# A decoder layer on one core: k and v of linear attention in a bank each, rows turned before the numerators, and v's copy and the gate's maxima in other slots of cross attention

## The chip, the cores and the metric

One core of a Trainium2 chip runs the whole program. The metric is the device time of one execution in microseconds. The kernel before took 587.42, 587.35 and 584.94 us in three runs, a median of 587.35.

## What is computed

The reference, cut to what matters (128 batches of 64 tokens, 128 features, 16 heads of 8; each block sits in a residual sum with a norm):

```python
# linear attention, then a feed-forward part whose activation is looked up on a grid of 0.1
h = _layernorm(x, ln1_g, ln1_b)
q, k, v = (h @ wq), (h @ wk), (h @ wv)             # each split in 16 heads
phi_q = jax.nn.elu(q) + 1.0
phi_k = jax.nn.elu(k) + 1.0
kv = jnp.einsum('bshd,bshe->bhde', phi_k, v)
z = jnp.sum(phi_k, axis=1)
out = (num / den).reshape(B, S, D)                 # num = phi_q kv, den = phi_q z + 1e-6
x = x + out @ wo
x = x + _lookup_act(_layernorm(x, ln2_g, ln2_b) @ w1) @ w2
# cross attention over ctx with a causal mask and a mask of query rows
scores = jnp.einsum('bhqd,bhkd->bhqk', q, k) / SQRT_DK
attn = jax.nn.softmax(jnp.where(m != 0, NEG, scores), axis=-1)
x = _layernorm(x + jnp.einsum('bhqk,bhkd->bqhd', attn, v).reshape(b, s, d) @ WO)
# shared expert plus a second expert weighted by the renormalised two best gates
out = xf @ W_shared.T + (w0 + w1) * (xf @ W_expert.T) + bias
x = _layernorm(x + out)
```

## The kernel before

The 8192 tokens are 64 tiles of 128 rows, in 16 groups (`NG`) of four tiles (`TG`). Everything stays in SBUF between three stages: `phase1` is linear attention, `phase2` the feed-forward part, `phase3` cross attention and the experts. Each stage is a software pipeline written out by hand: `pipeline(engine, phase)` calls the phase for step s = -1 to 16 and beyond on each of the five engines, and a step works on several groups at once (g = s + 1 is being opened, s is worked on, r = s - 1 or s - 2 is being closed). Each engine runs its own list in order; semaphores tie the lists together (`wait_ge`, and `after`, which leaves the wait out for a count of zero). PSUM has eight banks, `bank(i)`, in four pairs.

**Linear attention, one step.** TensorE's order is: turn the finished attention of group s - 1 (bank 0); the kv sums of s (`kv_products`, L1067, banks 2 and 3); q of g (L1125, bank 1); the numerators of s (`numerators`, L1083, banks 4 and 5); turn the normed rows of s + 2 (`xpose_rows`, L1054, bank 0); k and v of g by one product of 256 columns a tile (L1136), in banks 6 and 7 together, two tiles in each; the output projection of r (L1145, bank 1). VectorE masks the sums (`kv_sum`, L833), divides (`attend`, L844 to L850), makes phi_q (L877, reads bank 1), takes the minimum of Exp(k) and 1 (L881), makes phi_k (L887, reads k in PSUM, and waits also for v's copy, since v lies in the same banks), and takes the next group's statistics (L290, L297). ScalarE copies the projection and the turned attention, takes Relu and Exp of q, makes hT from the turned rows (L587), takes Exp of k (L634) and copies v (L638), both once `kv_done` says that all four products are there. GpSimd adds the residual and norms the rows.

**Cross attention, one step.** Four slots, one a tile; the tiles are alternately wide (64 keys a query, even slots) and narrow (32 keys, odd slots). In each slot TensorE closes the scores of the tile after (`scores_close`, L1213), turns the tile's probabilities (`turn_probabilities`, L1245), opens the scores of the tile two on (`scores_open`, L1231; it waits for ScalarE's copy of the turned probabilities, since it takes over their banks) and weighs the values (`weigh_values`, L1257, L1264, L1273). Between these stand: in slot 0 the fourth expert product of s - 2 (`moe`, L1301; it waits for the first collect, whose bank 5 it takes), the turning of y of g (bank 4), k of g (L1282, bank 5), the turning of the attention of r (L1345, bank 6); in slot 1 the output projection of r (L1328, bank 6) and q of g (bank 4); in slot 2 v of g (`project_v`, L1293, bank 4); in slot 3 the turning of y2 of r (bank 6) and, last, expert products 0 to 2 of r, in banks 5, 4 and 6 (`MOE_BANK`). These three wait for y2's copy, for v's copy out of bank 4 and for k's copy out of bank 5.

ScalarE's slot: copy the tile's turned probabilities (`copy_pT`, L726), then the exponentials of the next tile (`probabilities`, L719, which wait for VectorE). Around these: in slot 0 first the fourth collect (`collect`, L733) and y's copy (`copy_y`, L687), then the turned probabilities, then k's copy (L699) and the attention's (L755); in slot 1 last q's copy (L693); in slot 2 the gate's Exp (L750) and last v's copy (`copy_v`, L707); in slot 3 y2's copy (L759), the exponentials, and then collects 0 to 2.

VectorE's slot: `shift` of the next tile (its scores' maxima, L934, and their subtraction, L940 or L947), then `xattend` of this tile (L922, L924), which waits for its weighed values. Around these: in slot 1 the residual sum (L1017), its statistics, and the gate's maxima (`gate_top`, L956 to L961; it waits for all four collects of s - 2); in slot 2 first the mask rows of g (`future_keys`, L1004), later the gate's weights; in slot 3 the experts' mixture (L992) and the last norm's statistics. GpSimd: spread k over the heads (`spread_k`, L514), add the bias, norm y2 (L327), spread v (`spread_v`, L526), norm the output. SyncE loads mask rows and ctx two groups ahead (the mask load waits for `future_ready` of the step before) and stores the output.

Of the kernel before, what the change touches and what calls it, by code (L numbers as in the profile page):

```python
# [44 lines left out]
MOE_BANK = [5, 4, 6, 5]  # L45
# [7 lines left out]
def decoder_layer(nc, x, ctx, mask, mask_early, ln1_g, ln1_b, wq, wk, wv, wo, ln2_g, ln2_b, w1, w2,  # L53
# [15 lines left out]
    with es:  # L69
# [132 lines left out]
        q_done, kv_done = sem("q_done"), sem("kv_done")  # L202
# [375 lines left out]
        def _(act):  # L578
# [25 lines left out]
            def phase1(s, p):  # L604
# [25 lines left out]
                if exists(g):  # L630
                    act.wait_ge(kv_done, g + 1)
                    after(act, phik_ready, g - 1)
                    kv = pair[3][:, :, :].rearrange("p a (t c) -> p (a t) c", c=2 * D)
                    nc.scalar.activation(expqk[q][:, 1, :].rearrange("p (t d) -> p t d", d=D),  # L634
                                         kv[:, :, 0:D], ACT.Exp).then_inc(expk_ready, 1)

# [3 lines left out]
                        kv[:, :, D:2 * D].rearrange("p t (h e) -> p t h e", e=DH), ACT.Copy)\  # L640
# [96 lines left out]
            def phase3(s, p, slots=range(TG)):  # L737
                nxt, prev, q = s + 1, s - 1, 1 - p
                for t in slots:
                    if t == 0 and exists(s - 2):  # L740
                        collect((s - 2) * TG + TG - 1, TG - 1, p)
                    if t == 0 and exists(nxt):
                        copy_y(nxt)
                    if exists(s):
                        copy_pT(s * TG + t, t % 2)
# [10 lines left out]
                    if t == TG - 1 and exists(prev):  # L756
                        act.wait_ge(y2_xposed, prev + 1)
                        after(act, moe_done, prev * TG)
                        nc.scalar.activation(y2T[:, :], bank(6), ACT.Copy).then_inc(y2T_ready, 1)  # L759
                    if exists(s) if t < TG - 1 else exists(nxt):  # L760
                        probabilities(s * TG + t + 1)
# [5 lines left out]
                    if t == 2 and exists(nxt):  # L767
                        copy_v(nxt, q)
# [26 lines left out]
        def _(dve):  # L795
# [68 lines left out]
            def phase1(s, p):  # L864
# [9 lines left out]
                if exists(g):  # L874
# [9 lines left out]
                    dve.wait_ge(v_ready, g + 1)  # L884
                    after(dve, kvsum_done, g - 1)
                    kv = pair[3][:, :, :].rearrange("p a (t c) -> p (a t) c", c=2 * D)
                    nc.vector.scalar_tensor_tensor(  # L887
                        phi_k[q][:, :, :], kv[:, :, 0:D], 1.0,
                        expqk[q][:, 1, :].rearrange("p (t d) -> p t d", d=D), ALU.add, ALU.max)\
                        .then_inc(phik_ready, 1)  # L890
# [117 lines left out]
            def phase3(s, p, slots=range(TG)):  # L1008
                prev, old, q = s - 1, s - 2, 1 - p
                for t in slots:  # L1010
                    if t == 2 and exists(s + 1):
                        future_keys(s + 1, q)
# [12 lines left out]
                    if t == 1 and exists(old):  # L1025
                        dve.wait_ge(moe_ready, (s - 1) * TG)
                        gate_top(old, p)
                    if t == 2 and exists(old):
# [11 lines left out]
            phase3(-1, 1, slots=(2, 3))  # L1040
# [7 lines left out]
        def _(pe):  # L1048
# [3 lines left out]
            def transposes(src, dst, done):  # L1052
                for t in range(TG):
                    last = nc.tensor.transpose(dst[:, P * t:P * (t + 1)], src[:, t, :], ident[:, :])  # L1054
                last.then_inc(done, 1)

# [359 lines left out]
```

## Time and profile before

| What | Value |
|---|---|
| Median of three runs | 587.35 us (584.94 to 587.42) |
| The profiled execution | 587.63 us, its span 585.9 us |
| Busy share of the span | PE 88%, weight loads 62%, VectorE 71%, ScalarE 61%, GpSimd 59% |
| Chain that ended last | PE 51%, VectorE 26%, "issue" 10%, ScalarE 9% |
| Linear attention | about 9 to 137 us |
| Feed-forward part | about 125 to 254 us |
| Cross attention and experts | about 254 to 586 us |

The three stages have different limits, so the shares of the whole span say little; the rows of one step are read instead. PE is TensorE's matmul, PEld its weight load. An fp32 product appears as two records. In a timeline a bracket at the end of a row tells how long the engine stood idle before it and who ended that; rows of one engine can overlap by about 0.1 us, since each includes its own drain.

### The profile page before, as it was taken

To read this page: it belongs to the slowest core of one execution; us is meant where nothing else is said; L and a number is where in the kernel's file an instruction comes from. 1 tells how busy PE (TensorE), PEld (TensorE's weight loads), DVE (VectorE), ACT (ScalarE), POOL (GpSimd) and SP (SyncE) were. 2 spreads that over 40 slices of the span, in tenths; PEclk is the share of its full clock that TensorE was granted. 3 is DMA by queue.
4 is the path that set the end of the run, shared out by engine and by line. 5 is a ranking of instruction groups with operands and counts; after the bars stand their busy time and mean duration, and the time that the engine had idled before them with its cause. 6 is when DMAs were issued, how large, how long until landed. Compare 5 with 4: busy or idle time off the path is not lost.

```text
span 585.9 us, 23209 instructions
## 1 busy us (share of the span) xinstructions
PE 515.8 (88%) x9440; PEld 365.5 (62%) x9440; DVE 417.7 (71%) x1468; ACT 358.2 (61%) x643; POOL 346.4 (59%) x666
## 2 busy tenths in 40 slices
PE   3799999898999999988999999999999999998741
PEld 1566666665777777665666666666666666766530
DVE  2677677765777667556768787889888898888843
ACT  2455565556777777747657666666667666666420
POOL 6566666645577766631546557565766567665463
PEclk9999999999999999998999899999999999999875
DMA  5530000000000000010101012101111021100001
GB/s 160 163 109 3 2 2 2 2 2 1 2 0 2 2 2 2 0 30 29 32 3 45 5 50 49 47 8 45 48 49 32 20 49 48 48 21 4 22 18 36
DMA packets 24730, 17.45 MB, mean 30 GB/s; under 512 B 2096, under 2 KB 22448, under 8 KB 24624
## 3 DMA queue, kind: packets, MB, share of 16 engines
q1 hardware_dynamic: 24192, 15.90, 9.7%
q8 instruction: 75, 1.23, 0.9%
q14 instruction: 31, 0.25, 0.2%
q10 hardware_dynamic: 432, 0.07, 0.1%
HBM read 11.77 MB, written 4.19 MB: 27 GB/s over the span
## 4 chain that ended last, share of the span: by engine, by line
PE 51%; DVE 26%; issue 10%; ACT 9%; POOL 1%; DVEq 1%; DMA 1%; POOLq 0%; ACTq 0%
PE pair L1199 9%; PE pair L1163 9%; PE pair L1301 7%; DVE neg_max L934 5%; PE pair L1136 5%; PE pair L1054 5%; DVE gel L947 4%; PE pair L1213 3%; DVE stats_b L290 3%; PE pair L1245 3%; DVE stats L290 2%; PE pair L1282 2%; ACT v L707 2%; PE pair L1083 2%; PE pair L1273 2%
## 5 line engine op out<-in xcount | busy, mean ns | idle before, releaser
L719 ACT ACTIVATE gel<-gel,row_scale 128x512 f32<-128x512 f32 x96 | 66.0, 718 | 55.8 <-DVE gel L947 31.4
L726 ACT ACTIVATE gel<-pair 128x1024 f32<-128x1024 f32 x64 | 51.9, 811 | 42.7 <-PE pair L1245 42.3
L1213 PE MATMUL pair<-k_exp,qT 32*32 32x128 f32 (+1 forms) x2048 | 68.5, 328 | 0.0
L1199 PEld LDWEIGHTS pair<-w,gel 128*128 128x128 f32 x512 | 60.4, 192 | 8.0 <-issue 5.7
L1199 PE MATMUL pair<-w,gel 128*128 128x128 f32 x512 | 62.5, 276 | 1.0 <-ACT gel L652 1.0
L934 DVE TENSOR_REDUCE neg_max<-pair 128x16 f32<-128x1024 f32 x64 | 60.9, 951 | 1.8 <-PE pair L1213 1.5
L1245 PE MATMUL pair<-ident,gel 128*128 128x128 f32 x384 | 56.4, 283 | 5.9 <-ACT gel L719 5.9
L1163 PE MATMUL pair<-hT,w 128*128 128x512 f32 x128 | 58.2, 595 | 1.3 <-ACT lev L647 1.3
L1245 PEld LDWEIGHTS pair<-ident,gel 128*128 128x128 f32 x384 | 42.5, 143 | 23.4 <-ACT gel L719 13.2
L514 POOL TENSOR_SCALAR k_exp<-k_sb,quad_mask 128x512 f32<-128x512 f32 x64 | 43.0, 690 | 12.2 <-ACT k_sb L699 6.7
L305 POOL TENSOR_SCALAR veps_b<-mv_b 128x4 f32<-128x4 f32 x32 | 7.7, 242 | 65.0 <-DVE mv_b L297 32.1
L1054 PE MATMUL pair<-ident,xn 128*128 128x128 f32 x192 | 31.6, 290 | 15.7 <-POOL xn L327 15.7
L947 DVE TENSOR_TENSOR gel<-pair,neg_max 128x512 f32<-128x512 f32 x64 | 41.2, 686 | 1.1
L526 POOL COPY v<-v 32x256 f32<-32x256 f32 x64 | 26.2, 409 | 26.3 <-ACT v L707 23.4
L491 POOL TENSOR_TENSOR X<-X,proj_sb 128x512 f32<-128x512 f32 x16 | 20.3, 1270 | 36.1 <-ACT proj_sb L609 36.1
L922 DVE RECIPROCAL rec<-pair 128x16 f32<-128x16 f32 x64 | 15.9, 248 | 36.1 <-PE pair L1273 34.4
L1301 PE MATMUL pair<-w_moe,y2T 128*128 128x263 f32 x128 | 40.6, 448 | 0.7 <-ACT y2T L759 0.7
L1163 PEld LDWEIGHTS pair<-hT,w 128*128 128x128 f32 x128 | 22.9, 190 | 23.8 <-issue 23.5
L305 POOL TENSOR_SCALAR veps_c<-mv_c 128x4 f32<-128x4 f32 x16 | 3.7, 228 | 55.4 <-DVE mv_c L297 44.9
L652 ACT ACTIVATE gel<-lev 128x512 f32<-128x512 int8 x64 | 36.3, 620 | 0.1
L307 POOL TENSOR_TENSOR rstd_b<-veps_b,minus_half 128x4 f32<-128x4 f32 x32 | 34.6, 1082 | 2.7
L290 DVE BATCH_NORM_STATS2 stats<-X 128x6 f32<-128x128 f32 x128 | 27.6, 280 | 10.6 <-DMA X<-in_x 10.6
(127 smaller groups left out, 1251.9 us busy)
## 6 DMA issues: line engine op xcount, KB each, us to landing
X<-in_x SPq DMA_DIRECT2D x16, 256.0 KB, 3.1
cT<-in_ctx SPq DMA_DIRECT2D x16, 256.0 KB, 3.8
out_rows<-X SPq DMA_DIRECT2D x16, 256.0 KB, 2.5
mask_rows<-in_mask_early SPq DMA_DIRECT2D x16, 128.0 KB, 3.9
w<-in_L_attn_w SPq DMA_DIRECT2D x2, 256.0 KB, 3.4
w_kv<-in_L_attn_wk SPq DMA_DIRECT2D x1, 64.0 KB, 2.9
w_kv<-in_L_attn_wv SPq DMA_DIRECT2D x1, 64.0 KB, 2.6
w_q<-in_L_attn_wq ACTq DMA_DIRECT2D x1, 64.0 KB, 2.8
```

What stands on the lines that cost most here:

```text
L290: last = nc.vector.bn_stats(stats[:, t, :], rows(t))
L514: last = nc.gpsimd.tensor_scalar(k_exp[q][:, h, :], k_sb[:, :], quad_mask[:, h:h + 1], 0.0, ALU.mult, ALU.add)
L719: nc.scalar.activation(part, part, ACT.Exp, scale=row_scale[:, n:n + 1])\
L726: nc.scalar.activation(pT[par], flat[:, 0:GW] if n % 2 else flat, ACT.Copy)\
L934: nc.vector.tensor_reduce(neg_max[par][:, :].rearrange("p (a h) -> p a h", a=2), scores, AX.X, ALU.max, negate=True).then_inc(max_ready, 1)
L947: nc.vector.tensor_tensor(rows[:, heads, :], scores[:, half, :, :], neg_max[par][:, heads].unsqueeze(2).broadcast_to([P, HH, S]), ALU.add) ...
L1054: last = nc.tensor.transpose(dst[:, P * t:P * (t + 1)], src[:, t, :], ident[:, :])
L1163: nc.tensor.matmul(bank(up_bank(s, f)), w_1[:, P * f:P * (f + 1)], hT[p][:, :], start=True, stop=True).then_inc(up_done, 1)
L1199: last = nc.tensor.matmul(bank(6 + q)[:, P * t:P * (t + 1)], gel[:, q, f, P * t:P * (t + 1)], w_2[:, f, :], start=(f == 0), stop=(f == NF ...
L1213: last = nc.tensor.matmul(pair[t % 2][b * QW:(b + 1) * QW, quad // 2, heads], qT[p][rows, batch + first:batch + first + QW], k_exp[p][rows ...
L1245: last = nc.tensor.transpose(flat[:, P * i:P * (i + 1)], probability_rows(n)[:, P * i:P * (i + 1)], ident[:, :])
L1301: nc.tensor.matmul(bank(MOE_BANK[t])[:, 0:2 * D + NE], y2T[:, P * t:P * (t + 1)], w_moe[:, :], start=True, stop=True).then_inc(moe_done, 1)
```

## The change

On linear attention: k and v are made by two sets of four products of 128 columns, k in bank 6 and v in bank 7, with a semaphore each. Exp(k) waits for k alone, v's copy for v, and phi_k no longer waits for v's copy. The rows of s + 2 are turned before the numerators of s. On cross attention: TensorE turns slot 0's probabilities before y; ScalarE copies the turned probabilities before y; v's copy moves from the end of slot 2 to slot 3, behind y2's copy and before the exponentials; VectorE takes the gate's maxima and the mask rows in slot 0, between the next tile's shift and the attend, instead of slots 1 and 2; expert products 1 and 2 swap banks 4 and 6, and only the third waits for v's copy. The waits that guard banks 4 and 6 in slot 0 swap their counts.

```diff
-MOE_BANK = [5, 4, 6, 5]
+MOE_BANK = [5, 6, 4, 5]
 ...
@@ ScalarE, phase1
-                    act.wait_ge(kv_done, g + 1)
+                    act.wait_ge(k_done, g + 1)
                     after(act, phik_ready, g - 1)
-                    kv = pair[3][:, :, :].rearrange("p a (t c) -> p (a t) c", c=2 * D)
-                    nc.scalar.activation(expqk[q][:, 1, :].rearrange("p (t d) -> p t d", d=D),
-                                         kv[:, :, 0:D], ACT.Exp).then_inc(expk_ready, 1)
-
+                    nc.scalar.activation(expqk[q][:, 1, :], bank(6), ACT.Exp)\
+                        .then_inc(expk_ready, 1)
+                    act.wait_ge(v_done, g + 1)
                     after(act, kvsum_done, g - 1)
                     nc.scalar.activation(
                         v_ext[q].rearrange("p t (h e) -> p t h e", e=HV)[:, :, :, 0:DH],
-                        kv[:, :, D:2 * D].rearrange("p t (h e) -> p t h e", e=DH), ACT.Copy)\
+                        bank(7).rearrange("p (t h e) -> p t h e", t=TG, e=DH), ACT.Copy)\
                         .then_inc(v_ready, 1)
@@ ScalarE, phase3
+                    if exists(s):
+                        copy_pT(s * TG + t, t % 2)
                     if t == 0 and exists(nxt):
                         copy_y(nxt)
-                    if exists(s):
-                        copy_pT(s * TG + t, t % 2)
 ...
+                    if t == TG - 1 and exists(nxt):
+                        copy_v(nxt, q)
                     if exists(s) if t < TG - 1 else exists(nxt):
                         probabilities(s * TG + t + 1)
 ...
-                    if t == 2 and exists(nxt):
-                        copy_v(nxt, q)
@@ VectorE, phase1
                     dve.wait_ge(mink_ready, g + 1)
-                    dve.wait_ge(v_ready, g + 1)
                     after(dve, kvsum_done, g - 1)
-                    kv = pair[3][:, :, :].rearrange("p a (t c) -> p (a t) c", c=2 * D)
                     nc.vector.scalar_tensor_tensor(
-                        phi_k[q][:, :, :], kv[:, :, 0:D], 1.0,
-                        expqk[q][:, 1, :].rearrange("p (t d) -> p t d", d=D), ALU.add, ALU.max)\
-                        .then_inc(phik_ready, 1)
+                        phi_k[q].rearrange("p t d -> p (t d)"), bank(6), 1.0, expqk[q][:, 1, :],
+                        ALU.add, ALU.max).then_inc(phik_ready, 1)
@@ VectorE, phase3
-                    if t == 2 and exists(s + 1):
-                        future_keys(s + 1, q)
 ...
-                    if t == 1 and exists(old):
+                    if t == 0 and exists(old):
                         dve.wait_ge(moe_ready, (s - 1) * TG)
                         gate_top(old, p)
+                    if t == 0 and exists(s + 1):
+                        future_keys(s + 1, q)
 ...
-            phase3(-1, 1, slots=(2, 3))
+            future_keys(0, 0)
+            phase3(-1, 1, slots=(3,))
@@ TensorE, phase1
+            def rows_product(dst, src, w):
+                for t in range(TG):
+                    last = nc.tensor.matmul(dst[:, P * t:P * (t + 1)], src[:, P * t:P * (t + 1)], w,
+                                            start=True, stop=True)
+                return last
 ...
-                if exists(s):
-                    numerators(s, p)
                 if exists(s + 2):
                     xpose_rows(s + 2, p)
                 if s + 2 == NG:
                     xpose_rows2(0, p)
+                if exists(s):
+                    numerators(s, p)
                 if exists(g):
                     after(pe, phik_ready, g)
-                    for t in range(TG):
-                        last = nc.tensor.matmul(
-                            pair[3][:, t // 2, 2 * D * (t % 2):2 * D * (t % 2 + 1)],
-                            hT[q][:, P * t:P * (t + 1)], w_kv[:, :], start=True, stop=True)
-                    last.then_inc(kv_done, 1)
+                    rows_product(bank(6), hT[q], w_kv[:, 0:D]).then_inc(k_done, 1)
+                    after(pe, v_ready, g)
+                    rows_product(bank(7), hT[q], w_kv[:, D:2 * D]).then_inc(v_done, 1)
@@ TensorE, phase3
-                    if t == 0 and exists(g):
-                        after(pe, moe_ready, (s - 1) * TG - 2)
-                        after(pe, v2_ready, g)
-                        turn_y(g)
                     if s == 0 and t == 0:
                         scores_close(1)
                     if exists(s):
                         turn_probabilities(s * TG + t, t)
+                    if t == 0 and exists(g):
+                        after(pe, moe_ready, (s - 1) * TG - 1)
+                        after(pe, v2_ready, g)
+                        turn_y(g)
 ...
                         pe.wait_ge(xatt_ready, r * TG + TG)
-                        after(pe, moe_ready, (s - 1) * TG - 1)
+                        after(pe, moe_ready, (s - 1) * TG - 2)
 ...
                         if exists(g):
-                            pe.wait_ge(v2_ready, g + 1)
                             pe.wait_ge(k_ready, g + 1)
                         for u in range(TG - 1):
+                            if u == 2 and exists(g):
+                                pe.wait_ge(v2_ready, g + 1)
                             moe(r, u)
```

## Rows read from the trace of the kernel before

**Rows 1.** Busy times of one cross-attention step: us, engines, PEclk (granted clock), DMA
```profile
388.72:407.39 18.67, 17.52 (x457) 12.19 (x456) 15.62 (x54) 12.29 (x23) 11.94 (x23) 1.00 0.14 40
```

**Rows 2.** The chain of waits, its longest pieces: start, length, work
```profile
21.71 1.74 PE pair L1136 x8
...
120.97 1.74 PE pair L1136 x8
...
292.29 1.53 PE pair L1301 x6
...
310.97 1.53 PE pair L1301 x6
...
349.89 1.53 PE pair L1301 x6
...
536.67 1.53 PE pair L1301 x6
```

**Rows 3.** Timeline of a linear-attention step: start, length, engine, line, work, idle before
```profile
95.32 0.69 DVE L887 SCALAR_TENSOR_TENSOR arena<-pair,arena 128x512 f32<-128x512 f32 x1
...
96.73 1.12 PE L1125 MATMUL pair<-hT,w_q 128*128 128x512 f32 x2
...
97.34 0.73 DVE L833 TENSOR_TENSOR arena<-pair,head_mask 128x576 f32<-128x576 f32 x1
...
98.12 0.73 PE L1083 MATMUL pair<-arena 64*64 64x72 f32 x32 [0.27 <-DVE arena L833]
...
98.78 0.66 PE L1054 MATMUL pair<-ident,xn 128*128 128x128 f32 x4
...
99.28 1.89 PE L1136 MATMUL pair<-w_kv,hT 128*128 128x256 f32 x8
...
100.44 0.68 DVE L877 SCALAR_TENSOR_TENSOR arena<-pair,arena 128x512 f32<-128x512 f32 x1
...
101.23 1.13 PE L1145 MATMUL pair<-w_o,attT 128*128 128x128 f32 x8
...
101.84 0.43 DVE L881 TENSOR_SCALAR arena<-arena 128x512 f32<-128x512 f32 x1 [0.71 <-ACT arena L634]
...
102.19 0.60 PE L1054 MATMUL pair<-ident,att 128*128 128x128 f32 x4
```

**Rows 4.** Timeline of a cross-attention step, from the fourth expert product on
```profile
389.09 0.71 PE L1301 MATMUL pair<-w_moe,y2T 128*128 128x263 f32 x2
...
389.84 0.39 ACT L733 ACTIVATE moe_out<-pair 128x263 f32<-128x263 f32 x1 [0.39 <-PE pair L1301]
...
393.98 0.26 DVE L922 RECIPROCAL rec<-pair 128x16 f32<-128x16 f32 x1 [1.61 <-PE pair L1273]
...
399.29 0.34 DVE L956 MAX8 top<-moe_out 128x8 f32<-128x8 f32 x4
...
400.73 0.68 DVE L934 TENSOR_REDUCE neg_max<-pair 128x16 f32<-128x512 f32 x1
...
401.31 1.73 POOL L327 TENSOR_SCALAR xn<-X,negm_b,rstd_b 128x128 f32<-128x128 f32 x4 [0.18 <-POOL negm_b L322]
...
402.80 1.26 ACT L707 ACTIVATE v<-pair 64x512 f32<-64x512 f32 x2
...
402.95 0.66 PE L1245 MATMUL pair<-ident,gel 128*128 128x128 f32 x4 [0.42 <-ACT gel L719]
...
404.09 0.60 ACT L726 ACTIVATE gel<-pair 128x512 f32<-128x512 f32 x1
...
404.58 0.59 ACT L759 ACTIVATE y2T<-pair 128x512 f32<-128x512 f32 x1
...
404.74 0.30 PE L1231 MATMUL pair<-causal_bf,ident_bf 32*32 32x256 bf16 x8 [0.70 <-ACT gel L726]
...
405.95 1.33 ACT L719 ACTIVATE gel<-gel,row_scale 128x512 f32<-128x512 f32 x2 [0.78 <-DVE gel L947]
```

**Rows 5.** Busy times and granted clock where the clock fell, as [rows 1]
```profile
329.70:332.70 3.00, 3.00 (x38) 2.11 (x27) 2.57 (x11) 2.09 (x4) 0.06 (x1) 0.56 0.01 3
```

More of the change, by code:

```diff
@@ L201, in decoder_layer @@
         xn_xposed, hT_ready = sem("xn_xposed"), sem("hT_ready")
-        q_done, kv_done = sem("q_done"), sem("kv_done")
+        q_done, k_done, v_done = sem("q_done"), sem("k_done"), sem("v_done")
         expq_ready, expk_ready, v_ready = sem("expq_ready"), sem("expk_ready"), sem("v_ready")
@@ L1143, in phase1 @@
                     after(pe, projsb_ready, r)
-                    for t in range(TG):
-                        last = nc.tensor.matmul(bank(1)[:, P * t:P * (t + 1)],
-                                                attT[:, P * t:P * (t + 1)], w_o[:, :],
-                                                start=True, stop=True)
-                    last.then_inc(proj_done, 1)
+                    rows_product(bank(1), attT, w_o[:, :]).then_inc(proj_done, 1)
                 if s + 2 == NG + 1:
```

## The prediction

> **What bounds the kernel now.** I read the busy shares of one step of cross attention first [rows 1], then the chain of waits for the places where its pattern repeats [rows 2], then the timeline of one step in each of the two stages that the diff touches [rows 3, 4]. In linear attention TensorE and VectorE both stand idle in every step (the brackets in [rows 3]), so a loop through several engines sets the pace. In one step of cross attention (388.72 to 407.39) TensorE is busy 17.5 of 18.67 us: the most that orders and waits can give back there is the rest, 1.1 us. The feed-forward stage between them is untouched.
>
> The k/v products stand on the chain once a group: from 21.71 to 120.97 us, 14 periods of 7.09 us [rows 2]. The loop in [rows 3]: numerators (98.12), rows turned (98.78), k/v products (99.28, 1.89 us), ScalarE's Exp of k (inside the 0.67 us from the products' end, 101.17, to the minimum), VectorE's minimum (101.84, having stood idle 0.71 us for that Exp), phi_k, the next statistics, kv_sum (97.34 in this period), numerators. In cross attention the shared expert products stand on the chain at 292.29 and, 13 steps on, at 536.67: 244.4 us. One of the 13 held a fall of the clock [rows 5], worth 1.6 us (below); the others take (244.4 - 1.6)/13 = 18.67 us. TensorE stands idle twice in such a step, 0.42 us ahead of turning slot 3's probabilities and 0.70 us ahead of opening the next scores [rows 4].
>
> **Part 1: k and v in a bank each, rows turned before numerators.** The eight 256-column records become sixteen of 128 columns. Eight such records with stationary 128x128 are in the rows: the output projection runs from 101.23 to the next matmul at 102.19, 0.96 us. The old form takes at most 101.23 - 99.28 = 1.95 us, some of which is a wait for phi_q (it ends 101.12). So k is ready after about 1.1 us with its drain in place of 1.89, v after 2 x 0.96 = 1.92. TensorE pays between 0 and 0.25 us a step; I take 0.2 and it lies in a wait, as follows.
>
> Count from the start of the numerators, n (98.12). VectorE ends phi_q at 101.12, n + 3.0, whatever happens to k: its den, reciprocal and att hang on the numerators alone. k's Exp is now done by then: numerators 0.66, k 1.1, Exp and its waits 0.67, together n + 2.4 (ScalarE comes to it after the hT copy, which also moves forward with the turned rows). The 0.71 us of idle go. What is late next: the projection needs phi_q's bank, so it starts at n + 3.11 as now; k and v, from n + 0.66 to n + 2.6, fit ahead of it. Then 0.96 to the turned attention (n + 4.07), 0.50 to the kv sums (four transposes: 98.78 to 99.28; n + 4.57), 0.66 to q (the sums have as many products of the same shape as the numerators, 98.12 to 98.78; n + 5.23), about 0.88 for q (it ended 0.27 us ahead of the numerators, so its 1.12 holds its drain; n + 6.11), 0.50 for the rows that are now turned here (n + 6.61). So TensorE's own order gives a period of 6.61 us. VectorE's side: phi_q ends n + 3.0, minimum 0.43, phi_k starts n + 3.56 and kv_sum 2.02 later (95.32 to 97.34), n + 5.58, numerators 0.78 later at n + 6.36 (97.34 to 98.12). The moved transposes therefore cost 0.25 us against VectorE's bound, since they stand ahead of the numerators; they need only xn and bank 0, both long free, so they add no wait. phi_k (n + 4.25) is ready for the kv sums. Part 1 gives 7.09 - 6.61, 0.47 to 0.48 us in each of 15 periods: 7.1 us. Bounds: 6.36 (TensorE's row starts overlap better than I count) gives 11 us; nothing, if k's product is no earlier, gives 0.
>
> The Trainium skill speaks against this split: "TensorE: Matmul & The Clock Gate", section Back-to-back issue gap, says that at small widths the weight load is no longer hidden (some 81 ns sustained a matmul at 128 columns against 56 alone, for another data type). The rows give 0.12 us a 128-column record with its load, against some 0.22 for one of 256, so most of the load is hidden; by the page's ratio, 1.45, my estimate is that k and v would take 2.8 us in place of 1.92 and end past n + 3.11, at n + 3.45, and the period would be 6.95, 0.34 longer than I take; rival (c) below is its extreme.
>
> **Part 2: the slots of cross attention.** VectorE loses the gate's maxima and future's mask from the stretch ahead of slot 3's scores. From the first maximum (399.29) to the scores' maximum (400.73) are 1.44 us; the attend between them, a reciprocal (0.26 at 393.98) and a product that I take at 0.3, stays; so slot 3's scores start about 0.9 us earlier. Both land in slot 0, where VectorE stands idle 1.61 us ahead of 393.98. They need the 0.9 us that they free, up to 1.2 where nothing overlaps, so 0.4 to 0.7 us of cover are left; without cover they would cost their 0.9 to 1.2 in the main chain. The new wait for all four collects stands ahead of future's mask and the attend; the last collect lands at 390.23 (389.84 + 0.39) and VectorE comes there at 392.37 (393.98 - 1.61). SyncE's mask load waits for future's mask of the step before, which is now earlier: nothing. The exponentials of slot 3 then end before TensorE is free for them, and the 0.42 us go.
>
> v's copy (1.26 us at 402.80) leaves the place ahead of slot 3's transposed copy. That copy started at 404.09; now it starts when the transposes end. Let M be the start of the fourth expert product (389.09). TensorE is ready for slot 3's probabilities at 402.95 - 0.42, M + 13.4; their 0.66 end at M + 14.1, and ScalarE's copy runs there. y2's transposes need GpSimd's rows (401.31 + 1.73 = 403.04), M + 14.0, and take 0.6; its copy starts at M + 14.65. Now v's copy: 0.5 later, M + 15.15, 1.26 long. Queued behind it: the exponentials of the next tile (until now at 405.95, M + 16.86, waiting for VectorE), which start at M + 16.35 and end M + 17.65, then the first collect (0.39, starting 0.1 before their end), M + 18.0. The fourth expert product waits for this collect. So the period is 18.0 us, and of TensorE's 1.12 us 0.67 are gained and some 0.3 to 0.4 return as a new wait ahead of the fourth expert product. The swap of banks 4 and 6 leaves only the third expert product waiting for v's copy, at about M + 16.9 against M + 16.4: nothing. copy_y behind the transposed copy costs nothing that I can see: its reader, q's projection, stands in the next slot, and k's copy behind it feeds GpSimd, which is still busy with a norm then. 13 x 0.67 = 8.7 us. Bounds: all idle goes, 17.55 us, 14.5 us in all; none goes, 0. I take the loop, since every term has its row.
>
> Steps 0, 1 and 15 and the approach carry the same edits with other partners. VectorE's 0.9 in step 15 is on the chain; in step 0 slot 3's copy no longer stands behind v's. I take 1.8 us for them together, from 0 to 3. The tail's last chain (y2, experts, gate, norm) keeps its order.
>
> **The clock.** At 329.70 to 332.70 the granted clock is 0.56, against 1.00 in the steps around [rows 1, 5]: mostly the lower of the two levels, 1.2 GHz, behind a stretch with both idle times. Around it two steps of the chain take 349.89 - 310.97 = 38.92 us, and 38.92 - 2 x 18.67 = 1.6 us are lost. I keep one such loss.
>
> The Trainium skill's page "TensorE: Matmul & The Clock Gate", Part 1, says that activity releases the throttle; by that rule fewer idle times would spare that fall, and the trace agrees only in that the fall follows idle times.
>
> **The sum**: 7.1 + 8.7 + 1.8 = 17.6 us from the profiled execution's 587.6 (span 585.9), 570.0. That execution stands 0.3 us above the median of the three runs, less than the terms are known to.
>
> **Rivals.** (a) The waits dissolve: ScalarE's pieces overlap more than I count and the fourth expert product does not wait. For it: the y2 copy, v's copy and the exponentials are three terms whose overlap I read as 0.1 each. Price 0.3 to 0.45 a step, 5 us more, and perhaps the 1.6 of the clock: 564. (b) v's copy becomes the bound: it stands on ScalarE ahead of the exponentials in a loop with no spare; if 0.6 us more lies there (the y2 copy waits longer for GpSimd), cross attention gains nothing: 587.6 - 7.1 - 1.8 = 578.7. Against: GpSimd's start hangs on the sum of slot 1, whose order does not change. (c) Linear attention gives nothing, since the split's loads or the earlier transposes delay the numerators by 0.47 us: 577. (d) The change misses its aim and another loop holds both stages: within 3 us of 587. (e) Slower: the clock. The new wait stands apart from the old ones, after the expert products; if the clock fell in every step of cross attention and not in one of 14, 13 falls more at 1.6 us are 20.8 us, 17.6 are gained, and the time is 591. It decides from eleven falls more. Against: the step of [rows 1] has both idle times and keeps 1.00, and only one fall shows in the spacing of 13.
>
> **How the numbers follow.** Forecast 0.58 (566 to 574 by itself), (a) 0.15, (b) 0.08, (c) 0.08, (d) 0.06, (e) 0.05. The likeliest is 570. The range 563 to 579 holds the forecast, (a), (b) and (c). A difference under 0.5% is about what a measurement of this kernel can't tell from none: faster 0.89, same 0.06, slower 0.05.
>
> **What would show it.** Right: k/v products 6.6 us apart in the chain; no idle of VectorE ahead of the minimum; the numerators directly behind the turned rows. Cross attention 18.0 us a step; no 0.42 ahead of slot 3's transposes; a wait of ScalarE's collect ahead of the fourth expert product; v's copy, then exponentials, in the chain; VectorE's 1.61 us shrunk to 0.4 to 0.7. Wrong: VectorE idle ahead of the maxima in slot 0, a granted clock below 1.00 in more than two steps, or a wait of TensorE for v ahead of the third expert product.

## The result and the profile after

The changed kernel takes 572.38 us (median of four runs, 571.74 to 573.05), the kernel before beside it 587.38 (584.94 to 589.57): 0.975 of its time, 95% interval 0.971 to 0.979. The forecast was 570.0 with a range of 563 to 579. Its profiled execution took 573.05 us with a span of 571.3, 14.6 less than the span of before.

| Stretch of the profiled execution | before | after | gained |
|---|---|---|---|
| start to the first down projection of the feed-forward part | 138.52 | 131.93 | 6.6 |
| from there to step 1's expert products | 153.70 | 151.38 | 2.3 |
| from there to step 14's, 13 steps | 244.38 | 238.70 | 5.7 |
| step 15 and the tail, to the end of the span | 49.3 | 49.3 | 0 |

Linear attention, the timeline of one step (start, length, engine, line, work, idle before and its releaser). In the changed kernel the products of k and v and the projection stand on L1056, both turnings on L1051, and the numerators on L1086:

```profile
99.44 0.60 PE L1051 MATMUL pair<-ident,xn 128*128 128x128 f32 x4
...
99.97 0.73 PE L1086 MATMUL pair<-arena 64*64 64x72 f32 x32
...
100.64 2.05 PE L1056 MATMUL pair<-w_kv,hT 128*128 128x128 f32 x16
...
102.89 0.42 DVE L880 TENSOR_SCALAR arena<-arena 128x512 f32<-128x512 f32 x1
...
103.08 1.13 PE L1056 MATMUL pair<-w_o,attT 128*128 128x128 f32 x8 [0.39 <-issue]
...
105.23 1.13 PE L1128 MATMUL pair<-hT,w_q 128*128 128x512 f32 x2
...
106.20 0.60 PE L1051 MATMUL pair<-ident,xn 128*128 128x128 f32 x4
...
106.73 0.73 PE L1086 MATMUL pair<-arena 64*64 64x72 f32 x32
```

The idle time ahead of the minimum [rows 3] is gone (102.89 has no bracket), the numerators stand straight behind the turned rows, and the loop is TensorE's own list: numerators at 99.97 and 106.73 are 6.76 us apart. Of the 15 such periods the first two take 6.27 and 6.80 us, the next 12 take 6.74 to 6.76, and the last one 7.17.

Cross attention, the timeline of one step from its fourth expert product to the next one's:

```profile
377.57 0.71 PE L1298 MATMUL pair<-w_moe,y2T 128*128 128x263 f32 x2 [0.45 <-ACT moe_out L732]
...
382.46 0.26 DVE L918 RECIPROCAL rec<-pair 128x16 f32<-128x16 f32 x1 [0.58 <-PE pair L1270]
...
390.95 0.66 PE L1242 MATMUL pair<-ident,gel 128*128 128x128 f32 x4
...
392.25 0.60 ACT L758 ACTIVATE y2T<-pair 128x512 f32<-128x512 f32 x1
...
392.29 0.30 PE L1228 MATMUL pair<-causal_bf,ident_bf 32*32 32x256 bf16 x8
...
392.74 1.26 ACT L706 ACTIVATE v<-pair 64x512 f32<-64x512 f32 x2
...
394.03 1.33 ACT L718 ACTIVATE gel<-gel,row_scale 128x512 f32<-128x512 f32 x2
...
395.39 0.95 ACT L732 ACTIVATE moe_out<-pair 128x263 f32<-128x263 f32 x3
...
395.83 0.71 PE L1298 MATMUL pair<-w_moe,y2T 128*128 128x263 f32 x2 [0.44 <-ACT moe_out L732]
```

Both idle times of [rows 4] are gone ahead of L1242 and L1228. In their place the fourth expert product at 395.83, 18.26 us after the one at 377.57, waits 0.44 us for the first collect. VectorE's 1.61 us ahead of slot 0's attend are 0.58 here. The chain of waits, three of its pieces in that step (start, length, work), goes through v's copy as forecast:

```profile
393.35 0.66 ACT v L706
...
394.66 0.41 ACT gel L718
...
395.39 0.40 ACT moe_out L732
```

Whom TensorE waited for, in all of 300 to 500 us (engine, line, releaser, total, times, longest), first before, then after:

```profile
PE pair L1231 <- ACT gel L726: 7.4, 11, 0.7
PE pair L1245 <- ACT gel L719: 3.4, 9, 0.4
PE pair L1273 <- issue: 0.8, 2, 0.6
```

```profile
PE pair L1298 <- ACT moe_out L732: 4.6, 11, 0.4
PE pair L1270 <- issue: 0.5, 1, 0.5
PE pair L1228 <- ACT gel L725: 0.5, 2, 0.3
```

Of 10.8 us of waits for ScalarE's copies and exponentials 0.5 are left, and 4.6 are new, in eleven places.

### The profile page after: what moved, and what is told of

It reads as the page before. It is cut to its first block, busy times and chain, and to the rows that moved or that the text cites. A ratio compares the mean times of both kernels' runs of the same rounds, so it can differ in the third digit from the quotient of the medians.

```text
span 571.3 us, 23478 instructions
## 1 busy us (share of the span) xinstructions
PE 514.6 (90%) x9568; PEld 371.0 (65%) x9568; DVE 425.5 (74%) x1468; ACT 358.6 (63%) x643; POOL 347.7 (61%) x666
## 4 chain that ended last, share of the span: by engine, by line
PE 74%; ACT 9%; DVE 7%; issue 7%; POOL 3%; DMA 1%; DVEq 0%; POOLq 0%; ACTq 0%
PE pair L1196 10%; PE pair L1160 9%; PE pair L1056 8%; PE pair L1242 7%; PE pair L1210 6%; PE pair L1051 6%; PE pair L1279 4%; PE pair L1270 3%; PE pair L1128 3%; ACT v L706 3%; PE pair L1298 3%; PE pair L1290 2%; PE pair L1228 2%; PE pair L1325 2%; ACT gel L718 2%
## 5 line engine op out<-in xcount | busy, mean ns | idle before, releaser
L1242 PE MATMUL pair<-ident,gel 128*128 128x128 f32 x384 | 56.1, 282 | 2.4 <-ACT gel L718 2.4
L526 POOL COPY v<-v 32x256 f32<-32x256 f32 x64 | 26.6, 416 | 51.3 <-ACT v L706 48.3
L1242 PEld LDWEIGHTS pair<-ident,gel 128*128 128x128 f32 x384 | 42.2, 141 | 21.1 <-issue 15.3
L1051 PE MATMUL pair<-ident,xn 128*128 128x128 f32 x192 | 31.5, 289 | 16.1 <-POOL xn L327 16.1
L1051 PEld LDWEIGHTS pair<-ident,xn 128*128 128x128 f32 x192 | 23.4, 147 | 28.1 <-issue 17.0
L290 DVE BATCH_NORM_STATS2 stats<-X 128x6 f32<-128x128 f32 x128 | 27.6, 278 | 10.2 <-DMA X<-in_x 10.2
L307 POOL TENSOR_TENSOR rstd<-veps,minus_half 128x4 f32<-128x4 f32 x32 | 33.2, 1038 | 2.7
```

What stands on the lines that cost most here:

```text
L307: nc.gpsimd.tensor_tensor(rstd[:, :], veps[:, :], minus_half[:, :], ALU.pow)\
L1242: last = nc.tensor.transpose(flat[:, P * i:P * (i + 1)], probability_rows(n)[:, P * i:P * (i + 1)], ident[:, :])
```

## The experiments

Ten further kernels ran, each timed in three rounds beside the kernel before. The table gathers what all of them gave; the spacings are those that repeat most in the profiled execution. The kernel before had a median of 587.2 us beside the first four (lin_only, cross_only, split_only, rows_only), 585.8 beside the next four (gate_only, no_gate, v_back, moe_late) and 587.1 beside the last two, so across these sets the ratios are to be compared, and differences of 1 us in the medians mean little.

| Kernel | median us | ratio to before, 95% | linear period | cross step |
|---|---|---|---|---|
| before | 587.2 | 1 | 7.07 | 18.68 |
| after | 572.4 | 0.975 (0.971 to 0.979) | 6.75 | 18.26 |
| lin_only | 579.9 | 0.989 (0.987 to 0.992) | 6.75 | 18.68 |
| cross_only | 580.7 | 0.991 (0.988 to 0.993) | 7.07 | 18.28 |
| split_only | 573.7 | 0.978 (0.975 to 0.982) | 6.31 | 18.68 |
| rows_only | 582.7 | 0.993 (0.991 to 0.996) | 6.77 | 18.68 |
| gate_only | 576.4 | 0.982 (0.978 to 0.987) | 7.07 | 17.75 |
| no_gate | 579.4 | 0.986 (0.982 to 0.991) | 6.75 | 18.67 |
| v_back | 567.2 | 0.966 (0.963 to 0.970) | 6.75 | 17.74 |
| moe_late | 570.0 | 0.971 (0.967 to 0.975) | 6.75 | 18.02 |
| split_vback | 561.7 | 0.960 (0.956 to 0.964) | 6.31 | 17.75 |
| split_gate | 563.8 | 0.962 (0.959 to 0.965) | 6.31 | 17.75 |

**Each part alone.** lin_only is the kernel before with the linear-attention hunks of the diff, cross_only with those of cross attention.

> The kernel before with the whole linear-attention part of the change and nothing of cross attention. Theory (the two parts add): the period of linear attention is 6.75 us as in the changed kernel, against 7.09, the feed-forward part starts 6.6 us earlier and the time is 587.4 - 6.6 = 580.8, steps of cross attention stay at 18.67. Rival (the parts lean on each other, so that part of the 15 us comes only with both): the time differs from 580.8 by over 2 us.

> The kernel before with the whole cross-attention part of the change and nothing of linear attention. Theory (the parts add): linear attention 7.09 us a period, cross attention 18.26 us a step with a 0.45 us wait ahead of the fourth expert product, 587.4 - 8.0 = 579.4 (6.4 us of it from the steps and their edges, 1.6 from the fall of the clock that is not there). Rival: the fall of the clock comes back with the other timing, 581.

They gave 579.9 and 580.7 us, 7.4 and 6.5 less than before; together 13.9, against 15.0 for both. The parts add within the spread of before (584.7 to 590.1 in those runs). The spacings are the forecast ones to 0.02 us. cross_only lies 1.3 above what its theory gave. In its profiled execution the granted clock is 1.00 in each of the 13 steps of cross attention (three of them take 18.6 to 18.9 us all the same), so the fall that the rival names did not come back there. The difference stands at the start: from q's first product to its third cross_only takes 16.2 us and before 14.8, and q's second product takes 2.08 us in the one and 1.12 in the other, as explained below for rows_only.

**Which of the two edits of linear attention.** Both start from lin_only. split_only puts the rows back behind the numerators; rows_only is the other half, with the shared banks of before and the rows ahead.

```diff
 # split_only, TensorE, phase1, against lin_only
-                if exists(s + 2):
-                    xpose_rows(s + 2, p)
-                if s + 2 == NG:
-                    xpose_rows2(0, p)
                 if exists(s):
                     numerators(s, p)
+                if exists(s + 2):
+                    xpose_rows(s + 2, p)
+                if s + 2 == NG:
+                    xpose_rows2(0, p)
```

> The kernel before with k and v in a bank each, but the rows still turned behind the numerators. Theory A (the moved rows are what sets the new period, since they stand ahead of the numerators on TensorE's list, and k is early enough without them): numerators, rows 0.53, k 1.1, Exp 0.65 end together about 2.9 us after the numerators' start, no later than phi_q at 3.0; v ends at 3.17, the projection starts there, and the loop closes at 6.3 to 6.4 us through kv_sum; 15 periods at 0.7 us, about 577. Rival B (k needs the moved rows; behind them it is late and VectorE waits for its Exp): the period lies between 6.75 and 7.0, the time at 581 or above.

> The kernel before with the rows turned ahead of the numerators, k and v still made together. Theory A: the joint products start 0.66 instead of 1.16 us behind the numerators, end at 2.6, Exp at 3.15, v's copy at 3.65, so phi_k is 0.35 later than in the changed kernel, which VectorE's side can bear; TensorE's order closes the loop at 6.7 to 6.8 us, as with both edits: about 581. Rival B (the split is what brings the gain, since phi_k waits for v's copy): the period stays at 7.0 or above, the time at 586 or above.

Both went the way of theory A, and the two edits turn out not to help each other: the split alone gives 13.5 us, with the moved rows 7.4 (split_only's span is 14.0 us shorter than before's: 11.6 of them stand ahead of the feed-forward part, 15 x 0.76 = 11.4 by the periods; 1.6 are a fall of the clock that of these two only before's profile holds, and 0.8 lie in the last stretch). The timeline of split_only:

```profile
81.97 1.12 PE L1127 MATMUL pair<-hT,w_q 128*128 128x512 f32 x2
82.12 0.74 DVE L832 TENSOR_TENSOR arena<-pair,head_mask 128x576 f32<-128x576 f32 x1
...
83.03 0.73 PE L1085 MATMUL pair<-arena 64*64 64x72 f32 x32
...
83.69 0.66 PE L1050 MATMUL pair<-ident,xn 128*128 128x128 f32 x4
...
84.18 1.95 PE L1055 MATMUL pair<-w_kv,hT 128*128 128x128 f32 x16
...
85.94 0.43 DVE L880 TENSOR_SCALAR arena<-arena 128x512 f32<-128x512 f32 x1
...
86.13 1.13 PE L1145 MATMUL pair<-w_o,attT 128*128 128x128 f32 x8
```

Count again from the start n of the numerators. TensorE goes from the numerators (83.03) through the rows and sixteen records of k and v (84.18, 1.95 us; their 16 weight loads run beside them) to the projection at 86.13, n + 3.10, just where phi_q releases it; nothing waits. In the changed kernel the same projection starts at n + 3.11, having stood idle for 0.39 us, because the rows went ahead of the numerators and left the room empty. Those rows are work that has to lie somewhere: behind the numerators they fill TensorE's wait for VectorE's attend, ahead of them they delay that attend. The rest of the loop is then VectorE's (kv_sum at 82.12, numerators right behind it).

rows_only closes its loop at 6.77 through TensorE's list too, with VectorE waiting 0.33 us for k's Exp:

```profile
83.25 0.60 PE L1054 MATMUL pair<-ident,xn 128*128 128x128 f32 x4
...
83.78 0.73 PE L1083 MATMUL pair<-arena 64*64 64x72 f32 x32
...
86.88 1.13 PE L1145 MATMUL pair<-w_o,attT 128*128 128x128 f32 x8 [0.44 <-issue]
...
87.10 0.43 DVE L881 TENSOR_SCALAR arena<-arena 128x512 f32<-128x512 f32 x1 [0.33 <-ACT arena L634]
```

Its median is 1.7 above theory A's figure. The first two periods differ between executions: they take 13.4 us together in lin_only and 16.8 in rows_only, counted from q's first product to its third, while the repeated periods agree to 0.02. Where q's product of the second step takes 1.12 us the clock has risen by then, where it takes 2.0 to 2.1 it has not: the granted clock is 1.00 from 18.4 to 20 us in lin_only and 0.50, the lower of the two levels, from 20 to 22 us in rows_only. First lin_only, then rows_only:

```profile
18.45 1.12 PE L1127 MATMUL pair<-hT,w_q 128*128 128x512 f32 x2
```

```profile
19.72 2.01 PE L1125 MATMUL pair<-hT,w_q 128*128 128x512 f32 x2
```

In the profiles of this case these two periods take 12.7 to 13.9 us in all kernels that have the split of k and v, and 14.8 (before), 16.2 (cross_only), 16.4 (gate_only) and 16.8 (rows_only) in those without it, so 1 to 2 us of a difference between two kernels can be the start's.

**Which of the edits of cross attention.** gate_only is the kernel before with VectorE's two moves alone; no_gate is the changed kernel with these two undone.

```diff
 # gate_only, VectorE, phase3, against before
-                    if t == 2 and exists(s + 1):
-                        future_keys(s + 1, q)
 ...
-                    if t == 1 and exists(old):
+                    if t == 0 and exists(old):
                         dve.wait_ge(moe_ready, (s - 1) * TG)
                         gate_top(old, p)
+                    if t == 0 and exists(s + 1):
+                        future_keys(s + 1, q)
```

> The kernel before with only the gate's maxima and the mask rows moved to slot 0 of cross attention; v's copy, y's copy, the banks and TensorE's order stay. Theory A (this move alone carries the gain, and v's copy in slot 2 then stands in front of nothing): the exponentials of slot 3 end 12.9 us after the fourth expert product, v's copy runs until 14.1, just when the turned probabilities are there; the next exponentials wait for VectorE until 16.1 and the step takes 17.8 to 17.9 us: about 576. Rival B (v's copy ahead of slot 3's turned copy still holds TensorE): the step keeps the 0.7 us wait and takes 18.3 or more, 581 or above.

> The changed kernel with the gate's maxima and the mask rows back in slots 1 and 2. Theory A: slot 3's probabilities come 0.9 later, TensorE waits 0.42 for them, v's copy still stands in the loop of slot 3, and a step takes 18.6 to 18.7 us: 572.4 + 13 x 0.4 = 577.6 or more. Rival B (v's copy's new place is worth something of its own): 18.3 to 18.4, within 2 us of 573.

Both came out as theory A has it. VectorE's moves alone bring the step to 17.75, below the 18.26 of the whole change; all the rest without them brings nothing (18.67, and 579.4 us against lin_only's 579.9). gate_only's profile also holds six steps of 18.0 to 18.7 among its 13. Their granted clock is 1.00, so it is not the clock; in three of the six TensorE stands still for 0.2 to 0.7 us with "issue" as the releaser, in a fourth a row of scores takes 0.99 us in place of 0.61 (last section), and the rest is open.

**What v's copy does.** v_back moves it back in the changed kernel and touches nothing else; moe_late leaves it and moves the fourth expert product behind the turned probabilities.

```diff
 # v_back, ScalarE, phase3, against after
-                    if t == TG - 1 and exists(nxt):
-                        copy_v(nxt, q)
 ...
+                    if t == 2 and exists(nxt):
+                        copy_v(nxt, q)
 # moe_late, TensorE, phase3, against after
-                    if t == 0 and exists(s - 2):
-                        pe.wait_ge(moe_ready, (s - 2) * TG + 1)
-                        moe(s - 2, TG - 1)
 ...
                     if exists(s):
                         turn_probabilities(s * TG + t, t)
+                    if t == 0 and exists(s - 2):
+                        pe.wait_ge(moe_ready, (s - 2) * TG + 1)
+                        moe(s - 2, TG - 1)
```

> The changed kernel with v's copy back at the end of slot 2. Theory A (the copy's new place is what makes the new wait ahead of the fourth expert product): the exponentials of the next tile start when VectorE has them, 16.1 us after the fourth expert product instead of 16.47, the step takes 17.8 to 17.9, the wait shrinks to 0.1, and the time is 572.4 - 5 = 567.4. Rival B (the copy's new place spares TensorE the 0.7 us wait): it comes back, 18.3 us or more, 573 or above.

> The changed kernel with the fourth expert product behind the turning of slot 0's probabilities. Theory A (the 0.45 us ahead of that product is the whole loss against the forecast): the turning fills the wait, the step takes 17.8 us, 567. Rival B (the product, its collect and what stands behind them on ScalarE are then late, above all the turned copy that the next opening needs): the wait reappears ahead of the opening of slot 2's scores, within 1 us of 572.4.

v_back took 567.2 us, 0.2 from theory A. Its timeline:

```profile
371.53 1.27 ACT L706 ACTIVATE v<-pair 64x512 f32<-64x512 f32 x2
...
372.15 0.66 PE L1242 MATMUL pair<-ident,gel 128*128 128x128 f32 x4
...
372.85 0.60 ACT L725 ACTIVATE gel<-pair 128x512 f32<-128x512 f32 x1
...
374.76 1.33 ACT L718 ACTIVATE gel<-gel,row_scale 128x512 f32<-128x512 f32 x2 [0.68 <-DVE gel L943]
...
376.00 0.93 ACT L732 ACTIVATE moe_out<-pair 128x263 f32<-128x263 f32 x3
...
376.53 0.71 PE L1298 MATMUL pair<-w_moe,y2T 128*128 128x263 f32 x2
```

v's copy ends at 372.80 and the turned copy starts at 372.85, right where slot 3's transposes end: with VectorE's moves made, the copy lies in time that ScalarE has free, and the exponentials (374.76) wait 0.68 us for VectorE. So the move of v's copy cures what VectorE's moves have already cured, and costs the 0.45 us ahead of the fourth expert product.

moe_late fell between its two theories: 570.0 us and 18.02 a step. The wait ahead of the fourth product is gone, and about half of it is back one place further:

```profile
377.39 0.61 PE L1298 MATMUL pair<-w_moe,y2T 128*128 128x263 f32 x2
...
377.84 0.60 PE L1051 MATMUL pair<-ident,X 128*128 128x128 f32 x4
378.04 0.39 ACT L732 ACTIVATE moe_out<-pair 128x263 f32<-128x263 f32 x1 [0.54 <-PE pair L1298]
...
378.53 1.10 PE L1279 MATMUL pair<-cT,w_xk 128*128 128x512 f32 x2
```

k's product at 378.53 takes over bank 5 and waits for the fourth collect (378.04 + 0.39 = 378.43), where y's four transposes at 377.84 would have left TensorE free by 378.3. The view gives no wait there; I read it from the times: k's product starts 0.69 us behind y's transposes, and 0.44 us behind them in v_back, and the step is longer than v_back's by about as much (18.02 against 17.74). I had looked for a new wait only at the openings.

**The two losses taken out, and the two edits alone.** split_vback is the changed kernel with the rows behind the numerators and with v's copy moved back, the diffs of split_only and v_back together. split_gate is the kernel before with k and v in a bank each and with gate_only's diff.

> The changed kernel with two of its moves undone: the rows are turned behind the numerators again, and v's copy stands at the end of slot 2. Theory (the two losses found are independent): linear attention 6.31 us a period, cross attention 17.75 a step, 567.2 - (579.9 - 573.7) = 561.0. Rival (TensorE's stalls without a visible cause, half a microsecond here and there once it has no other idle, eat part of it): 563 or above.

> The kernel before with two edits alone: k and v in a bank each, and the gate's maxima and the mask rows in slot 0. Everything else stays (order of rows and numerators, v's copy, y's copy and turning, banks). Theory (these two carry the gain, and everything else in the change costs or gives nothing): 573.7 - (587.2 - 576.4) = 562.9, 6.31 us a period and 17.75 a step. Rival (the swapped banks and TensorE's order in slot 0 give something of their own): 2 us or more above the kernel that has them and v's copy in slot 2.

split_vback took 561.7, 0.7 above the sum of the single results, and beats both kernels: 25.4 us below before, 10.7 below after. split_gate, two edits on the kernel before, took 563.8. Its theory took gate_only's gain against the 587.2 of another set; against the before beside gate_only the gain is 9.4 us and the sum is 564.3. split_gate lies 2.1 us above split_vback, at the edge that was named for the rival, and the ratios' intervals overlap. The shortest step is 17.75 in both, but it repeats in eight of split_vback's 13 steps and in five of split_gate's, which has steps of 18.6 and 19.3 too. Between 300 and 500 us TensorE waits for the copy of the turned probabilities ahead of opening scores six times in split_gate, 1.6 us together, and twice in split_vback, 0.5 us. That speaks for a small worth of the order of slot 0 or of the swapped banks; it isn't settled, since no run has one of these two alone.

## Why the prediction was right, step by step

The places were right, the sizes only in part, and the nearness of the total is partly luck. The two gains that repeat in every step were forecast as 7.1 + 8.7 = 15.8 us and gave 4.8 + 5.4 = 10.2. The profiled execution gained 14.6 all the same, because 4.4 us came from elsewhere: 2.3 from steps 0 and 1, 1.8 from the start of the kernel and one long period of before, and 1.6 from a fall of the clock that only before had, less 1.3 for steps of after that ran longer. n is the start of the numerators and M that of the fourth expert product, as in the prediction.

**Part 1, 7.1 us forecast.** The mechanism was right: k is early, VectorE no longer waits for its Exp, the projection stays at n + 3.11 and TensorE's list closes the loop. The size was off: 6.75 us, not 6.61. Two terms were too small: q's product to the next transposes takes 0.97 us (105.23 to 106.20) where I took 0.88 from the end of its drain, and each set of four transposes 0.53, not 0.50. And the 7.09 that I started from is a mean that holds one long period of 7.41; the period that repeats is 7.07. The period gives 7.07 - 6.75 = 0.32 in each of 15, 4.8 us. The rest of the table's 6.6 is mostly the first two steps, which take 12.7 us in place of 14.8, 1.4 more than the shorter period explains, and the 0.3 of before's long period; the same two steps take 12.7 to 13.9 in the kernels that share the changed order of linear attention, so part of the 1.4 is chance. The bound that I gave for VectorE's side, 6.36, is near what split_only reached (6.31): I took the difference to my 6.61 as the moved rows' cost, 0.25 a step, and it was in truth 0.44.

The price of the split was right: 1.92 us were forecast for k and v; the row of split_only has 1.95, 0.12 a record, and that of the changed kernel 2.05. The Trainium skill's ratio in "TensorE: Matmul & The Clock Gate", Back-to-back issue gap, gave an estimate of 2.8; the trace decides against carrying it over to this type.

**Part 2, 8.7 us forecast.** Every place was right: the 0.42 us gone, the 0.70 gone, a new wait ahead of the fourth expert product behind v's copy, the exponentials and the first collect. v's copy starts at M + 15.17 (forecast 15.15), y2's at M + 14.68 (14.65). The step is 18.26, not 18.0, because two handovers on ScalarE came without the overlap that I had counted: the exponentials start at M + 16.46 (394.03, 0.03 behind the end of v's copy) and the collects at M + 17.82 (0.03 behind the exponentials), where I took 16.35 and 17.55 from rows that overlap by 0.1. That leaves 5.4 of the 8.7 us. In v_back the collects do start 0.09 before the exponentials end. Why here not, I can't show.

**The edges, 1.8 forecast.** The stretch with steps 0 and 1 gave 2.3. Step 15 and the tail gave nothing, where I had counted VectorE's 0.9: slot 3's subtraction of the maxima starts only 0.17 us earlier against the expert products, and y2's rows, GpSimd's work, end at 538.23 and are what TensorE then waits for (its transposes start at 538.28, as far behind the expert products, 16.27 us, as before). That the step's own new wait took up the rest is my reading. This last stretch is not known to better than 0.8 us: it takes 49.3 us in before and 48.5 in lin_only, whose cross attention is the same.

**The clock, nothing forecast.** Here before lost 1.6 us that after did not lose, by luck as far as the runs show, and this helped to bring the sum back near the forecast: 5.7 us over 13 steps, of which 5.4 are the steps' (242.8 - 13 x 18.26) and 1.6 the clock's, less 1.3 for steps that ran longer, two of them 19.00 and 18.92 (last section). I had held fewer idle times as a possible reason for a spared fall, by the Trainium skill's page "TensorE: Matmul & The Clock Gate", Part 1. The runs don't bear that out for this fall: lin_only has the same waits in every step as before and no fall from 278 us on, as this view of busy times shows (the granted clock is the third number from the end), first before, then lin_only:

```profile
278.00:530.00 252.00, 238.65 (x6144) 165.47 (x6142) 204.12 (x678) 165.18 (x293) 154.70 (x296) 0.99 0.13 35
```

```profile
278.00:530.00 252.00, 237.49 (x6222) 165.32 (x6206) 208.38 (x699) 166.12 (x297) 156.81 (x303) 1.00 0.13 35
```

Its thirteen steps take 18.67 to 18.69, and so do those of split_only and rows_only. So with the same idle times the fall came in one of four profiles. What decides it isn't shown; 1.6 us of a difference between two kernels can be that.

**The rivals.** (a), (b), (c) and (d) fell; (b)'s place was right and its size small. (e) fell too: the granted clock is 1.00 in each of the 13 steps.

## What to carry to other kernels

When several edits aim at the same wait, cost each one with the others already made: here VectorE's move had freed the place, and moving v's copy as well only built a new queue ahead of the exponentials. Work that is moved off one engine's critical place needs a hole to lie in; look for the hole on both sides, since transposes ahead of the numerators cost 0.44 us a step and behind them nothing. Where a queue of instructions on one engine sets the end, don't take for granted the 0.1 us by which such rows overlap elsewhere. And when a total comes out near its forecast, compare the spacings that repeat: here they gave 10.2 of the 15.8 us that were forecast for them.

## What the runs showed of the hardware that I had not expected

TensorE has stalls that no view explains. In the changed kernel one weighing of values (L1270) stands still for 0.54 us with "issue" as its releaser, and its step takes 19.00 instead of 18.26:

```profile
353.73 0.30 PE L1270 MATMUL pair<-v,gel 128*32 128x18 f32 x11 [0.54 <-issue]
...
425.65 1.28 PE L1210 MATMUL pair<-k_exp,qT 32*32 32x256 f32 x16
```

The stall falls between the 53rd and the 54th of the 64 records of that weighing, in the fourth of the 13 steps, and it does so in ten of the twelve profiles, 0.45 to 0.81 us long, though the kernels reach that place at times from 347 to 365 us; lin_only and split_only don't have it. The long step of 18.92 has no idle time in the view, but its sixteen score records at 425.65 take 1.28 us where those at 389.14 take 0.61. The same records of the same, the eighth, step are long in seven profiles, 0.97 to 1.28 us. So both return at the same place of the program in most kernels and are not scattered chance. The cause isn't shown. Before has two stalls put to "issue" between 300 and 500 us, 0.8 us together, and its step at the first one still takes 18.69; where TensorE has hardly any idle left nothing hides them. v_back, moe_late and split_vback have two or three each in that stretch, 0.3 to 0.8 long. Here are split_vback's:

```profile
PE pair L1270 <- issue: 0.8, 1, 0.8
...
PE pair L1210 <- issue: 0.3, 1, 0.3
```

Halving the width of fp32 products costs little: the chain counts 1.74 us for the eight records of 256 columns in before [rows 2], 1.79 in split_only and 1.98 in after for sixteen of 128, each with its own weight load.

VectorE's mixture (L988, four instructions) takes 1.68 us in the changed kernel and 1.13 in v_back. In the first GpSimd spreads v at the same time (L526), in the second it had done so before. v_back differs by the place of v's copy alone, and the others agree: over all 64 instructions the mean is 446 to 466 ns with v's copy in slot 3 (after, cross_only, moe_late, no_gate) and 345 to 347 ns with it in slot 2 (before, v_back, gate_only). That the overlap with GpSimd is the reason is my reading; no run moves GpSimd's work alone. Whether it costs the step anything isn't shown either. First after, then v_back:

```profile
394.02 1.68 DVE L988 SCALAR_TENSOR_TENSOR moe_out<-moe_out,top_sum 128x128 f32<-128x128 f32 x4
...
394.17 1.87 POOL L526 COPY v<-v 32x256 f32<-32x256 f32 x4 [2.67 <-ACT v L706]
```

```profile
372.96 1.82 POOL L526 COPY v<-v 32x256 f32<-32x256 f32 x4 [0.23 <-ACT v L706]
...
375.24 1.13 DVE L988 SCALAR_TENSOR_TENSOR moe_out<-moe_out,top_sum 128x128 f32<-128x128 f32 x4
```
